# A graph network: the edge network of 28 of 98 window groups moved beside the message steps

## The reference

```python
h = relu(layernorm(x))
x = x + (segment_sum(h[src] * edge_weight[:, None], dst) @ W_neigh + b_neigh) + h @ W_self.T
h = relu(layernorm(x))                    # not used by the second layer but for its shape
s = segment_sum(edge_attr, src); m = segment_max(edge_attr, src); m = where(cnt > 0, m, 0)
h = concat([s, m, s / max(cnt, 1), u[batch]], axis=1)          # batch is 0 for every node
x = x + relu(h @ W1 + b1) @ W2 + b2
```

## Time and profile before

| what | us |
|---|---|
| median of 3 runs (lowest, highest) | 1921.56 (1917.66, 1940.19) |
| span of the profiled execution | 1898.8 |
| what lies around it, against the median | 22.8 |
| PE busy in the span | 1004.9 (53%) |
| DVE busy | 1274.2 (67%) |
| ACT busy | 743.8 (39%) |
| POOL busy | 1125.6 (59%) |

### The profile page before, as it was taken

One profiled execution on the slowest core, in us unless ns is written; L12 is line 12 of the kernel. 1 busy time (PEld: TensorE's weight loads), 2 busy tenths in 40 slices (PEclk: granted clock), 3 DMA queues, 4 the chain that ended last, 5 costly groups with the idle time before them and its releaser, 6 DMA issues. The chain is left out here.

```text
span 1898.8 us, 39252 instructions
## 1 busy us (share of the span) xinstructions
PE 1004.9 (53%) x13560; PEld 866.0 (46%) x13561; DVE 1274.2 (67%) x3119; ACT 743.8 (39%) x1962; POOL 1125.6 (59%) x1212
## 2 busy tenths in 40 slices
PE   1022445444444446432433332243599999999996
PEld 1011344443334435322323331242488888888885
DVE  3033667666656667544686664596699998999985
ACT  1001456555545556422222211132155554545553
POOL 7755445445464445466776676765066666666663
PEclk9975666666666666655555555566599999999997
DMA  9910133333333334322434442344399999999997
GB/s 283 167 21 11 43 76 83 77 78 77 76 66 76 79 77 93 75 62 70 120 99 105 111 109 73 77 114 111 98 207 221 222 215 205 214 213 222 210 210 95
DMA packets 521162, 229.67 MB, mean 121 GB/s; under 512 B 486253, under 2 KB 493677, under 8 KB 520285
## 3 DMA queue, kind: packets, MB, share of 16 engines
q0 software_dynamic: 162672, 98.52, 30.1%
q1 hardware_dynamic: 334606, 111.32, 28.1%
q10 hardware_dynamic: 23680, 17.25, 3.6%
HBM read 138.46 MB, written 88.33 MB: 119 GB/s over the span
## 5 line engine op out<-in xcount | busy, mean ns | idle before, releaser
L930 POOL DMA_INDIRECT by_win<-rows,idx_win x391 | 382.3, 978 | 355.7 <-DVE idx_win L366 233.9
L923 POOL DMA_INDIRECT xg_all<-in_x_dram,src_i x390 | 394.1, 1011 | 161.9 <-issue 117.0
L1308 PE MATMUL ps<-ident,h 128*128 128x128 f32 x588 | 142.9, 390 | 322.6 <-issue 115.0
L1481 POOL DMA_DIRECT2D out_dram<-rows x97 | 156.5, 1613 | 167.7 <-ACT rows L1655 167.7
L1308 PEld LDWEIGHTS ps<-ident,h 128*128 128x128 f32 x588 | 96.2, 200 | 343.5 <-issue 123.6
L1396 ACT ACTIVATE sq<-xc 128x512 f32<-128x512 f32 x147 | 92.5, 629 | 406.8 <-DVE xc L1040 270.9
L1321 PE MATMUL ps<-wsT,hT 128*128 128x128 f32 x784 | 167.7, 385 | 152.1 <-DVE arena L1090 93.3
L1321 PEld LDWEIGHTS ps<-wsT,hT 128*128 128x128 f32 x784 | 156.3, 295 | 157.2 <-issue 154.6
L1414 ACT ACTIVATE h<-xc,stat 128x64 f32<-128x64 f32 x784 | 196.3, 333 | 0.0
L482 ACT ACTIVATE hist<-ps 32x256 f32<-32x256 f32 x196 | 72.6, 371 | 246.9 <-remote 228.5
L1610 PE MATMUL ps<-w_sb,arena 128*96 128x64 f32 x1568 | 157.8, 254 | 8.8 <-issue 6.0
(11 more groups left out here) (204 smaller groups left out, 2567.7 us busy)
## 6 DMA issues: line engine op xcount, KB each, us to landing
rows<-flag_d POOLq DMA_DIRECT2D x98, 288.0 KB, 8.7
out_dram<-rows POOLq DMA_DIRECT2D x97, 256.0 KB, 9.3
rows<-message SPq DMA_DIRECT2D x588, 36.4 KB, 4.7
message<-m_row SPq DMA_DIRECT2D x48, 388.0 KB
arena<-in_x_dram SPq DMA_DIRECT2D x70, 256.0 KB
out_dram<-arena SPq DMA_DIRECT2D x70, 256.0 KB
rows<-slot_d POOLq DMA_DIRECT2D x98, 144.0 KB, 6.2
by_win<-zeros ACTq DMA_DIRECT2D x12, 808.5 KB
```

The costliest lines, as they stand in the source:

```text
L923: nc.gpsimd.indirect_dma_start(out=xg[g % RX][:, t % GT, :], out_offset=None, in_=x, in_offset=bass.IndirectOffsetOnAxis(ap=(src_i[:, t:t ...
L930: nc.gpsimd.indirect_dma_start(out=by_win, out_offset=bass.IndirectOffsetOnAxis(ap=idx_win[0:parts, t:t + 1], axis=0), in_=rows[0:parts, t ...
L1308: last = nc.tensor.transpose(hT_of[n % 2][:, P * k:P * k + P], h[n % 2][:, 2 * k:2 * k + 2, :].rearrange("p a c -> p (a c)"), ident[:, :])
L1481: pool.dma_start(nodes_of(out, g), y[b][:, :, :], accum_op=ALU.add).then_inc(summed_out[b], 16)
```

## The change

- **28 light groups.** The edge network of window groups 0 to 27 (LIGHT, the windows of the first two sort batches) is computed in the message stage. Job j's first half (permute, scans, both halves of the hidden layer, outer layer) stands in the edge step STARTS_AT[j]: two of three steps from 11 to 35, then each from 36 to 46. Its second half (value, parts, sums) stands in the step after. The hidden layer goes in two halves through the banks 6 and 7. ACT copies the sums to an SBUF tile and SP stores them to the new table edge_d, 256 KB each.
- **Window stage.** The 70 heavy groups come first, then the 28 light ones. A light group has its messages summed as before, and DVE adds the reloaded sums (e_in) to the bank instead of ACT's copy. The message pieces of light groups are split 4 and 4 between SP and ACT, and SP issues the reload.
- **Gathers.** 3 groups instead of 8 are gathered ahead of the scatters, 46 instead of 41 after them. Where node steps start beside the ranking stays at group 8.
- **Message stage.** All 16 left node steps come in the first four edge steps. The sorts start at step 3 + 5 n instead of 9 + 5 n.
- **Waits.** POOL waits for the attribute rows in three parts. Some semaphores are merged; the keys' PSUM bank is single.

The diff, cut to its core (lines of one engine's program that only rename are left out):

```diff
-                while todo and (MG - 1 - g) * left < len(todo) * (MG - 1):
+                while todo and (EARLY - g) * left < len(todo) * (EARLY + 1):
                     tail.append(todo.popleft())
...
+        EARLY = 3
+        FIRST_BESIDE = GT
...
-        SORT_AT = [EARLY + 1 + 5 * n for n in range(NB)]
+        SORT_AT = [EARLY + 5 * n for n in range(NB)]
...
+        GROUPS = list(range(LIGHT, WG)) + list(range(LIGHT))
+        BY_SYNC = [GT - 2] * HEAVY + [GT // 2] * LIGHT
+        STARTS_AT = [11 + 3 * j // 2 for j in range(17)] + list(range(36, MG - 2))
+        assert len(STARTS_AT) == LIGHT and STARTS_AT[16] < 36
+        first_half = {at: j for j, at in enumerate(STARTS_AT)}
+        second_half = {at + 1: j for j, at in enumerate(STARTS_AT)}
...
+        def edge_hidden_half(pe, g, half):
+            if half == 0:
+                pe.wait_ge(w["u"], g + 1)
+                if g >= 1:
+                    pe.wait_ge(w["v_all"], g)
+            else:
+                pe.wait_ge(w["hid"], 2 * g + 1)
+            for j, part in enumerate((sums, tops, means)):
+                for side in range(2):
+                    q = 2 * half + side
+                    last = nc.tensor.matmul(
+                        ps[6 + side][:, 0:2 * SL],
+                        w1r[DE * q:DE * q + DE, j, :],
+                        part[DE * q:DE * q + DE, :],
+                        start=(j == 0), stop=(j == 2), tile_position=(DE * q, 0))
+            last.then_inc(w["z"], 1)
...
+        def edge_finish(act, g):
+            act.wait_ge(w["o_ps"], g + 1)
+            if g >= 2:
+                act.wait_ge(edge_out[g % 2], 16 * (g // 2))
+            nc.scalar.activation(y[g % 2][:, :, :], o_node[:, :].rearrange("p (k c) -> p k c", c=D),
+                                 ACT.Copy).then_inc(w["y"], 1)
...
+                    which = attr_first if t == 0 else attr_second if t <= 3 * step_t else loaded["attr"]
...
+                        if g + 2 in first_half:
+                            job = first_half[g + 2]
+                            if job * GT % SB == 0:
+                                batch = job * GT // SB
+                                sp.wait_ge(order_out[batch % 2], 64 * (batch // 2 + 1))
+                            load_group(sp, job)
+                        if g in second_half:
+                            job = second_half[g]
+                            sp.wait_ge(w["y"], job + 1)
+                            sp.dma_start(edge_d[job], y[job % 2][:, :, :].rearrange("p k c -> p (k c)")).then_inc(edge_out[job % 2], 16)
...
+                    if t == 0:
+                        pool.wait_ge(attr_first, 16)
+                    if t == 4 * GT:
+                        pool.wait_ge(attr_second, 16 * 3)
+                    if t == 16 * GT:
+                        pool.wait_ge(loaded["attr"], 16 * (-(-FT // (4 * GT)) - 3))
...
+                    one = first_half.get(g) if kind == "edge" else None
+                    two = second_half.get(g) if kind == "edge" else None
...
+                    if one is not None:
+                        edge_permute(dve, one)
...
+                    if two is not None:
+                        edge_value(dve, two)
                     scale_of(n, 1)
...
                     next(sort, None)
+                    if two is not None:
+                        edge_left(dve, two)
+                    if one is not None:
+                        edge_scans(dve, own, one)
+                    if two is not None:
+                        edge_select(dve, two)
                     weigh(n - 1)
...
+                        edge_low(dve, two)
                     relu_of(n - 1)
...
+                    one = first_half.get(g) if kind == "edge" else None
+                    two = second_half.get(g) if kind == "edge" else None
...
+                    if one is not None:
+                        edge_permuted(pe, one)
                     step(step_of[kind, g])
+                    if one is not None:
+                        edge_hidden_half(pe, one, 0)
+                        edge_hidden_half(pe, one, 1)
+                    if two is not None:
+                        if two == 0:
+                            pe.wait_ge(ln["kept"], step_of["node", WG - 1] + 1)
+                        else:
+                            pe.wait_ge(w["y"], two)
+                        edge_sums(pe, o_node, two, True)
+                    if one is not None:
+                        edge_outer(pe, one)
                     if kind == "edge" and g in SORT_END:
                         n = SORT_END.index(g)
                         pe.wait_ge(srt["end"], n + 1)
...
+                def add(p):
+                    b, g = p % RING, GROUPS[p]
+                    dve.wait_ge(w["picked"], p + 1)
+                    dve.wait_ge(w["y"], LIGHT + p)
+                    dve.wait_ge(e_loaded[g % RING], 48 * len(range(g % RING, LIGHT, RING)) + 16 * nth(g))
+                    dve.wait_ge(summed_out[b], stored_from(b, p))
+                    nc.vector.tensor_tensor(y[b][:, :, :], ps[o_bank[p % 2]][:, :].rearrange("p (k c) -> p k c", c=D),
+                                            e_in[g % RING][:, :, :], ALU.add).then_inc(w["y"], 1)
```

More of the change, by code:

```diff
@@ new lines, in edge_permuted @@
+        def edge_permuted(pe, g):
+            b = g % RING
+            pe.wait_ge(w["perm"], g + 1)
+            if g >= 1:
+                pe.wait_ge(w["u"], g)
+            for s in range(2):
+                for q in range(4):
+                    k = 2 * q + s
+                    last = nc.tensor.matmul(pp_of(g)[DE * q:DE * q + DE, SL * s:SL * s + SL], a_in[b][0:SL, k, 0:DE],
+                                            perm[:, SL * k:SL * k + SL], start=True, stop=True,
+                                            tile_position=(0, DE * q))
+            last.then_inc(w["pp"], 1)
@@ new lines, in edge_outer, with edge_sums @@
+        def edge_outer(pe, g):
+            pe.wait_ge(w["hid"], z_count(g + 1))
+            if g >= 1:
+                pe.wait_ge(w["v_all"], g)
+            for k in range(GT):
+                last = nc.tensor.matmul(v_of(g)[0:SL, D * k:D * k + D], hid[:, SL * k:SL * k + SL], w2_sb[:, :],
+                                        start=True, stop=True)
+            last.then_inc(w["v_ps"], 1)
+        def edge_sums(pe, bank, g, opens):
+            pe.wait_ge(w["sel"], g + 1)
+            pe.wait_ge(w["v"], g + 1)
+            for k in range(GT):
+                for n in range(PARTS):
+                    last = nc.tensor.matmul(bank[:, D * k:D * k + D], sel[pair(g)][:, k, :], v_part[pair(g)][:, k, n, :],
+                                            start=(opens and k == 0 and n == 0), stop=(k == GT - 1 and n == PARTS - 1))
+            last.then_inc(w["o_ps"], 1)
@@ L1437, in _ @@
                 place_act(act, r_win, beside)
-                for st in tail_steps[:-1]:
-                    step(step_of[st])
+                for kind, g in tail_steps[:-1]:
+                    n = step_of[kind, g]
+                    one = first_half.get(g) if kind == "edge" else None
+                    two = second_half.get(g) if kind == "edge" else None
+                    if one is None and two is None:
+                        step(n)
+                        continue
+                    turned(n - 2)
+                    if two is not None:
+                        edge_high(act, two)
+                    square(n)
+                    relu(n - 1)
+                    if two is not None:
+                        edge_mid(act, two)
+                    if one is not None:
+                        edge_relu_half(act, one, 0)
+                        edge_relu_half(act, one, 1)
+                    root(n)
+                    if two is not None:
+                        edge_finish(act, two)
                 LAST = len(steps) - 1
@@ new lines, in _ @@
+                edge_permute(dve, LIGHT)
+                edge_scans(dve, own, LIGHT)
+                for p in range(HEAVY):
+                    g = GROUPS[p]
+                    if g + 1 < WG:
+                        edge_permute(dve, g + 1)
+                    if p >= 1:
+                        edge_value(dve, g - 1)
+                    picks(p)
+                    edge_select(dve, g)
+                    if p >= 1:
+                        edge_left(dve, g - 1)
+                    if g + 1 < WG:
+                        edge_scans(dve, own, g + 1)
+                    if p >= 1:
+                        edge_low(dve, g - 1)
@@ L1635, in _ @@
[L1635 to L1636 removed]
+                edge_permuted(pe, LIGHT)
+                for p in range(HEAVY):
+                    g = GROUPS[p]
                     hidden(g)
[L1638 to L1639 removed]
+                    if p >= 2:
+                        edge_sums(pe, ps[o_bank[p % 2]], g - 2, False)
                     if g + 1 < WG:
[L1641 to L1643 removed]
@@ L1710, in _ @@
-                value_high(WG - 1)
```

(17 more changed lines are left out.)

434 lines of the change are left out of this document (215 added, 219 removed).

## The result

The changed kernel takes 2058.67 us (median of 6 runs, 2047.74 to 2077.81) against 1917.04 for the kernel before (6 runs), ratio 1.074, 95% interval 1.0695 to 1.0789: slower, by 142 us where 101 were forecast. The two profiled executions lie further apart, 1898.8 and 2075.9 us of span, 177 us; each of the later runs, which list both, shows a time of 1.7 to 2 us over its span, so the 22.8 us that I put "around" the first span were spread between executions.

The account below looks back on a forecast made before the run. It took the message stage to be bound by no engine's work, with PE held up while POOL issues indirect DMAs. Start -60, message stage +185 and window stage -24 gave +101, so 2020 us, own range 1961 to 2085, overall 1840 to 2085.

Parts of the forecast that it names:

- quota of PE: Message stage and ranking: PE finishes some 60 matmuls, then none, while POOL issues indirect DMAs without a gap.
- The start, -60: Ranking: 24 gathers instead of 64 ahead of the scatters, so they start earlier; -60 us, between -40 and -75.
- The message stage, +185: Message stage with the 28 jobs added: 715 us against 530, +185; bounds +132 and +220.
- my own bound of +220: Message stage, upper bound of its growth: job steps in a row at 17 us instead of 14.7.
- steps 11 to 35: Message stage, two of three edge steps with a job: three steps priced at 44 us, 25 steps at 367.
- steps 36 to 40: Message stage, each edge step with a job under gathers: 16 us each, together 80.
- Steps 0 to 10: Message stage, with the 16 node steps: 324 matmuls at 1.5 to 1.8 per us under gathers, 190 us.
- The last part: Message stage after the gathers end near step 41: last eight steps at a job's chain of 9.7 us, together 78.
- The window stage, -24: Window stage: 28 light groups at 4.4 us instead of 5.26, -24 us, between 0 and -38.
- The clock: Message stage: PE's granted clock stays low, under 0.7; if lifted, job chains would be 84 us less.
- (C): Message stage rival: job chains fill the standstills, stage stays at 530 us; total -84, 1838 us; chance 0.27.
- (B): Message stage rival: idle time is fixed latency, DVE's 132 us add to it; total +48, 1970 us; chance 0.17.

Follow-up runs that it names:

- e7: Kernel before with a 128 x 256 memset on POOL behind each indirect DMA and one pacing semaphore instead of five: 1765.74 us, ratio 0.913.
- e5: Changed kernel with 11 extra matmuls where PE waits in a job's first half: 2070.17 us, ratio 1.071 to the kernel before.
- e10: Changed kernel with a 128 x 16 memset behind each indirect DMA and 11 extra matmuls per job: 1602.38 us, ratio 1.002 to the kernel before.
- Set 2: Changed kernel and kernel before run again as a pair, on a chip without standstills: 1621.4 against 1594.49 us, ratio 1.018.
- e4: Changed kernel with the message stage's 366 gathers replaced by plain transfers of consecutive rows: 1627.26 us, ratio 1.016 to the kernel before.
- e3: Changed kernel with POOL gathering at most four groups ahead of the edge steps instead of eight: 1625.53 us, ratio 1.013 to the kernel before.

## Why the prediction was right, step by step

**The standstills.** The forecast rested on what I called a quota of PE under unbroken indirect DMAs: the idle time of the message stage can't be used by added work. That was so in the result: none of the 143 us in which PE, DVE and ACT all stood was filled; where there are no standstills it fell from 174 (82 of it one wait for POOL to begin its gathers) to 48. e7 shows that they go with POOL's way of issuing. Two things I had wrong. I took them for a property of the kernel, and they are there in some sets only; without them the same change costs 1.8%, so some 110 of the 142 us go with the standstills. And the quota isn't a fixed number of matmuls: 56 in the opening run of 55 DMAs agrees with it, but in the job steps 24 gathers in a row let 184 through, 5.3 per us:

```profile
1181.70:1216.70 35.00, 22.38 (x184) 19.15 (x184) 25.56 (x72) 8.63 (x18) 27.99 (x24) 0.65 0.44 115
```

**The start, -60.** Measured -43.6: the 14 us of the second group's wait weren't gained, since the ranking stands still under 24 gathers too (PE's first 60 matmuls are done at 27.8 us, and none follows until 45). In the bounds.

**The message stage, +185.** Measured +261, outside my own bound of +220 and my sign of 680 to 750 us (it is 781). Ten of the 76 us come from 530, where the marks give 519.8. By the table above, steps 11 to 35, priced 367 from three ranking groups, took 373, and steps 36 to 40, priced 80, took 86. Steps 0 to 10, priced 190, took 220. The 330 matmuls there went at 1.5 per us, the low end of my 1.5 to 1.8; in the opening run of POOL into five free buffers it was 0.8 (56 in 69.5 us), while I had taken a mean of 1.7. The last part, priced 78, took 103. There I used PE's 4.4 us per job at the higher level of the clock, although I had said that I leave it low, and most job steps took 14.2 us where I had 9.7. With PE at the 7.7 us that I had for the lower level my own sum gives 13.0. (I also counted eight job steps; the last job starts in step 46.) So the mechanism held, and the mis-sized terms are these two.

**The window stage, -24.** Measured -35 and -5.5 at the end, together past my bound of -38. A light group takes 3.6 us, under the 3.9 that I got from bytes; by my own text that part was wrong. DVE's addition waits there for the accumulating store (52.7 us in all), which I had set as the reason for a smaller gain; why a light group still is faster than its bytes, no run tells.

**The total.** By the profiled pair the terms' misses add up to 76 us: 76 in the message stage, 16 at the start, -17 in the window stage with the end. By the medians the change costs 142 us, 41 more than forecast; the profiled pair, 177 us apart, joins the slowest of the six runs after with a span before that is shorter than any of the six times. So the time lies in the range because the mechanism and its sign were right and the range was wide, not because each term was. My own range of 1961 to 2085 was also narrower than the terms' bounds added, which give 1941 to 2102.

**The clock.** I left it low, and it stayed at 0.58. The rule that I set against it (the Trainium skill, "TensorE: Matmul & The Clock Gate", "Part 1: The HAM clock gate") has the gate open for a busy engine. The jobs' own matmuls didn't do it, with PE busy for 63.98 of 81 us at 0.56 in the last job steps; those that e5 and e10 put into the waits did, in part (0.75 and 0.73).

**Rivals.** (C) had the change faster if the standstills were ordinary waits. Set 2 is that case, without standstills, and it is still slower by 1.8%, for two reasons. The start gains 3.5 us and not 60, since POOL bounds the first two stages. And the message stage grows by 70 us: 65 of them lie in the steps with jobs, whose chains, where each step has a job, take 12.3 to 14.6 us at a granted clock of 0.56 to 0.61. e4 and e10 show that: without indirect gathers the stage stays as long, with a higher clock it gets shorter. (B), 1970, lay under the result. On the longer gathers (+28 us) the Trainium skill, "SBUF — State Buffer", "Who interferes with whom", has that DVE and GpSimd share a port pair, and that a DMA whose descriptors GpSimd makes can be starved by it. The 1.02 and 1.09 us per gather agree with that, though no run separates it. Its rule that PE waits on no one doesn't cover the standstills.

**Open.** What differs between the chips, by what way POOL's DMAs hold up PE, and whether the recording has a part in it, no run shows. Nor whether a gap between 0.31 and 0.49 us would do, what of the 98 us ahead of the first job is the order of the steps, and whether e3's shorter runs help where there are standstills.

## What to carry to other kernels

Look for stretches in which all engines stand still but the one that issues indirect DMAs. Don't count their idle time as room for moved work: here the three others stood for 143 us before and after. Before trusting such a stretch, run the kernel on another chip; here the loss was 7.4% in one place and 1.8% in another. Where the standstills are real, a short pause between the DMAs was worth its cost (149 us for some 320 in the kernel before); where they aren't, the same pause cost a tenth (the changed kernel, 1621 to 1782 us across two sets). And look at the clock of a chain before pricing it: 4.4 us of PE's work were 7.7 at the lower level by my estimate, and the steps bore it out.

## What the runs showed of the hardware that was not expected

- The same kernel before took 1594 to 1603 us in three sets and 1917 to 1936 in the result and one set, with the same DMA durations on POOL (median 958 ns for a scatter in both). The difference lies ahead of the window stage, which takes 509.0 and 507.1 us.
- In the traces with standstills a third of the records of semaphore updates is missing (27410 against 41792), nearly all ahead of the window stage.
- A memset between indirect DMAs, which widens the 0.30 us between them to 0.49, ends the long standstills (1936 to 1766 us).
- With 11 extra matmuls in its waits PE's clock was granted at 0.75 instead of 0.56, and a job step got shorter by up to a third although it held more work.
- Beside DVE's added work an indirect gather on POOL took 7% longer (1.019 and 1.090 us).
